# A two-layer language-model tower on one core: the recurrence's 8-column products streamed four times over

## What is computed

```
def _rnn_layer(inp, W_ih, W_hh, b_ih, b_hh):
    pre = jnp.einsum('bsi,hi->bsh', inp, W_ih) + (b_ih + b_hh)
    h0 = jnp.zeros((inp.shape[0], W_hh.shape[0]), dtype=inp.dtype)
    def step(h, p_t):
        h = jnp.tanh(p_t + h @ W_hh.T)
        return (h, h)
    _, hs = jax.lax.scan(step, h0, jnp.swapaxes(pre, 0, 1))
    return jnp.swapaxes(hs, 0, 1)
...
h = _rnn_layer(x, W_ih_0, W_hh_0, b_ih_0, b_hh_0)
h = _rnn_layer(h, W_ih_1, W_hh_1, b_ih_1, b_hh_1)
return h @ fc_w.T + fc_b
```

## Time and profile before

| what | value |
|---|---|
| median of 3 runs | 1154.31 us (1153.18 to 1155.77) |
| span of the profiled execution | 1152.6 us |
| PE busy | 1094.6 us, 95% |
| PE weight loads busy | 935.8 us, 81% |
| ACT busy | 787.2 us, 68% |
| DVE busy | 699.3 us, 61% |
| mean granted TensorE clock | 0.642 |
| L656, 8-column matmuls | 16384, 169 ns each |

### The profile page before, as it was taken

The page is one execution under the profiler, slowest core; times in us unless marked ns, Lnnn a source line. Parts: engine busy times, 40 slices in busy tenths (PEclk is TensorE's granted clock), DMA queues, the critical chain, the costliest instruction groups (busy, mean ns, idle before and its releaser), DMA issues.

```text
span 1152.6 us, 62476 instructions
## 1 busy us (share of the span) xinstructions
PE 1094.6 (95%) x26880; PEld 935.8 (81%) x26880; DVE 699.3 (61%) x3140; ACT 787.2 (68%) x4577; POOL 144.5 (13%) x220
## 2 busy tenths in 40 slices
PE   4799999999999999999999999999899879889998
PEld 2699999999999999999999999999744368823333
DVE  7565455555555555555555544444456769899996
ACT  1466777777777777777777777677567878666664
POOL 4200000000000000000000000000003302331210
PEclk9555555555555555555555555555599989999999
DMA  4000000000000000000000000000000000256686
GB/s 143 8 9 10 9 9 14 9 9 9 10 13 10 9 9 9 10 14 9 9 5 5 4 5 5 5 4 5 3 1 1 1 1 1 86 212 228 247 285 204
DMA packets 30594, 47.22 MB, mean 41 GB/s; under 512 B 12322, under 2 KB 21611, under 8 KB 30316
## 3 DMA queue, kind: packets, MB, share of 16 engines
q1 hardware_dynamic: 29772, 43.08, 11.2%
q10 hardware_dynamic: 544, 0.13, 0.0%
HBM read 40.84 MB, written 2.36 MB: 37 GB/s over the span
## 4 chain that ended last, share of the span: by engine, by line
PE 86%; DVE 5%; ACT 3%; POOL 2%; issue 2%; DMA 1%; SPq 1%; DVEq 0%; POOLq 0%; ACTq 0%
PE bank L656 44%; PE bank L752 7%; PE bank L1403 6%; PE bank L735 5%; PE bank L1708 5%; PE bank L426 4%; PE bank L525 3%; PE bank L730 2%; PE bank L1436 1%; PE bank L747 1%; PE bank L1585 1%; PE bank L411 1%; PE bank L446 1%; PE bank L315 1%; PE bank L1493 1%
## 5 line engine op out<-in xcount | busy, mean ns | idle before, releaser
L656 PE MATMUL bank<-space,whh_hi 128*128 128x8 f16 x16384 | 609.5, 169 | 7.4 <-DVE space L783 4.4
L656 PEld LDWEIGHTS bank<-space,whh_hi 128*128 128x128 f16 x16384 | 528.4, 105 | 25.3 <-DVE space L783 7.4
L783 DVE TENSOR_TENSOR space<-h_f,space 128x16 f16<-128x16 f32 x2048 | 291.5, 176 | 380.4 <-ACT h_f L764 378.8
L764 ACT ACTIVATE h_f<-bank 128x16 f32<-128x16 f32 x2048 | 300.1, 184 | 229.8 <-PE bank L656 222.4
L770 ACT ACTIVATE space<-bank 128x16 f16<-128x16 f32 x2048 | 299.0, 184 | 1.1 <-PE bank L656 1.1
L656 PE MATMUL bank<-space,whh_lo 128*128 128x32 f16 (+1 forms) x2096 | 145.0, 190 | 0.0
L752 PE MATMUL bank<-space,wih_hi 128*128 128x32 f16 x2048 | 137.1, 188 | 0.0
L426 PE MATMUL bank<-onehot,tab 128*128 128x128 f16 x448 | 116.7, 266 | 0.5 <-DVE prepare_cur L476 0.5
L735 PE MATMUL bank<-xr,wih_hi 128*128 128x32 f16 x512 | 109.8, 214 | 0.0
L730 PE MATMUL bank<-ones,bias 128*128 128x32 bf16 x512 | 102.9, 201 | 0.0
L656 PEld LDWEIGHTS bank<-space,whh_lo 128*128 128x128 f16 x2096 | 102.2, 107 | 0.0
(11 more groups left out here) (303 smaller groups left out, 1637.8 us busy)
## 6 DMA issues: line engine op xcount, KB each, us to landing
space<-weights_kept SPq DMA_DIRECT2D x64, 512.0 KB, 7.7
space<-in_x SPq DMA_DIRECT2D x28, 129.0 KB, 3.1
out<-res SPq DMA_DIRECT2D x7, 256.0 KB, 9.9
space<-in_wrec SPq DMA_DIRECT2D x1, 768.0 KB, 4.1
space<-in_wx SPq DMA_DIRECT2D x1, 740.5 KB, 9.0
brec<-in_brec SPq DMA_DIRECT2D x1, 260.0 KB
ew<-in_ew SPq DMA_DIRECT2D x1, 256.0 KB, 4.1
weights_kept<-wturned SPq DMA_DIRECT2D x8, 32.0 KB, 1.8
```

The source lines that it names most:

```text
L656: mm = pe.matmul(own[:, m, :], w[:, k, m * P:(m + 1) * P], steps(h, k), start=False, stop=False, skip_group_check=True)
L764: act.activation(h_f[layer][:, s % 2, :, :], own, ACT.Tanh, scale=scale[layer]).then_inc(s_h[layer], 1)
L783: dve.tensor_tensor(h[layer][:, :, s % RINGS[layer], 1, :], h_f[layer][:, s % 2, :, :], h[layer][:, :, s % RINGS[layer], 0, :], ALU.subtra ...
```

## The change

The four matmuls of each state product stream 32 columns in place of 8. The moving operand is the same 8 columns four times, read with a step of zero. The output goes to the 8 columns of the step's own sums and to three copies of them, at distances of 64, 128 and 192 columns in the same bank, which nothing reads. The products with `whh_lo`, the inputs, biases and all other matmuls are as before.

```diff
@@ -27,6 +27,7 @@
 OFF = 2 * U + 2
+COPIES = 4
 EPS = 1e-5
@@ -106,6 +107,11 @@
             return bank[layer * 3 + block % 3][:, 0:KH * U * B].rearrange("p (m s b) -> p m s b", m=KH, b=B)
+
+        def wide_sums(layer, s):
+
+            own = bank[layer * 3 + s // U % 3].rearrange("p (j m s b) -> p m s j b", m=KH, s=U, b=B)
+            return own[:, :, s % U, 0:COPIES, :]
@@ -657,14 +663,23 @@
             return mm
 
+        def add_wide(pe, own, w, state):
+
+            for m in range(KH):
+                for k in range(KH):
+                    mm = pe.matmul(own[:, m, :, :], w[:, k, m * P:(m + 1) * P],
+                                   state[:, k, :].unsqueeze(1).to_broadcast([P, COPIES, B]),
+                                   start=False, stop=False, skip_group_check=True)
+            return mm
+
         def rec_tensor(pe, g):
 
             def low(layer, s):
                 if 0 <= s < T:
                     pe.wait_ge(s_lo[layer], OPEN + s)
                     at = (s - 1) % RINGS[layer]
-                    add(pe, sums(layer, s // U)[:, :, s % U, :], whh_hi[layer], h[layer],
-                        lambda h, k: h[:, k, at, 1, :]).then_inc(s_sum[layer], 1)
+                    add_wide(pe, wide_sums(layer, s), whh_hi[layer],
+                             h[layer][:, :, at, 1, :]).then_inc(s_sum[layer], 1)
@@ -672,8 +687,8 @@
                     pe.wait_ge(s_hi[layer], OPEN + s)
                     at = (s - 1) % RINGS[layer]
-                    add(pe, sums(layer, s // U)[:, :, s % U, :], whh_hi[layer], h[layer],
-                        lambda h, k: h[:, k, at, 0, :]).then_inc(s_part[layer], 1)
+                    add_wide(pe, wide_sums(layer, s), whh_hi[layer],
+                             h[layer][:, :, at, 0, :]).then_inc(s_part[layer], 1)
```

## The result

The changed kernel takes **1140.85 us** (median of 4 runs, 1140.43 to 1142.36) against 1154.61 us before (4 runs): a ratio of 0.9882, with a 95% interval of 0.9868 to 0.9896. It is 1.2% faster. The forecast was 1136, with a range of 1126 to 1155. The span of its profiled execution, which took 1142.36 us and was the slowest of the four, is 1140.4 us. In what follows, one run of the kernel without L735 that took 1314.4 us, at a granted clock of 0.52 in place of 0.64, is left out of the figures.

A forecast was written before the change was run, and what follows sets the result against it. Main bound: the recurrence's 753 ns low loop, with PE's stream second. At 2.4 GHz, 1033 × (765.3 − 746) = 19.9 us, less 1.5, took the span from 1152.6 to 1134.2; plus 1.7, 1136 us, range 1126 to 1155.

The forecast's parts named there:

- The low loop: Recurrence's closed loop: four low-state products, tanh, subtraction, products again; claimed as main bound, about 753 ns a step.
- the stream: PE's sequence of products and filled-in matmuls in a recurrence step; claimed to cost 0.012 us a step, some 12 us.
- The clock: PE's granted clock in the recurrence; claimed to rise from 1.2 to 2.4 GHz soon after layer 1 starts and stay.
- the slower rival: Recurrence clock stays at 1.2 GHz, wider products add only latency: loop 773 ns, time 1168 us; chance 0.13.
- The loop at the high clock: Low-state product, tanh and subtraction loop at 2.4 GHz: claimed 746 ns a step, bounds 734 and 764.
- the first weight load: Load opening each burst of low products, at most 27 ns; claimed to halve at 2.4 GHz, −12 ns, bounds 0 and −13.
- The remainder of 1.5: Allowance of 1.5 us in all for waits at the recurrence's start, where the preparation holds up some steps.
- The signs that I named: Profile after: clock at 9 or 10 tenths, products at 176 ns, steps of 0.75, PE's subtraction waits among the longest.
- The layout rival: Copies' spaced output and zero-step operand cost two cycles a column: loop 763 ns, time 1153 us, no change; chance 0.06.
- the larger gain: Last matmul of a burst ends 10 ns earlier at 2.4 GHz: loop 728 ns, time 1117 us; chance 0.03.

## Why the prediction was right

**The bound, as read: right.** The low loop is 753.4 ns before and 750.5 after, and the stream stretched some steps above it: a third of that was taken away by itself in a run, and all of it went with the high clock. Split by the trace, the recurrence's 13.1 us are 1033 × (753.4 − 750.5) = 3.0 us of the loop and 1033 × (11.9 − 2.2) = 10.0 us of what lay above it. The larger part came from the smaller of the two bounds, since little of the loop depends on PE's clock. Three readings of the chain were loose and change nothing: the step at 405.37 has L735 three times and L747 twice, not L735 twice and L747 once, and the step at 404.64 has 7 matmuls behind its products and takes 0.73, that at 403.89 has 9.

**The clock: right, and decisive.** It rose at 49.1 us and stayed until 810.3. The steps ahead of that and the last ones ran at the low level with 32 columns, most of them at 773 to 774 ns, which is the loop the slower rival had. It also fell and rose again at the end of the recurrence, as foreseen. The forecast gave this 0.78 on an argument about how fully the array is fed; the outcome bears it out for these products, and the kernel with 16 columns shows that a smaller change would have missed.

**The loop at the high clock: the term that was mis-sized.** I had 746 and it is 750.5, so that of a forecast gain of 7 ns a step in the loop only 3 came. (The sum itself was off by one: 753 less 8 is 745, which would have made the forecast 1135.) By its parts: the gaps between the four matmuls went from 27 to 25 (−5 in all; −4 foreseen), the last matmul from 168 to 176 (+8; +8 foreseen), and the signals to and from DVE took 1 ns more each, with the tanh and the subtraction 1 ns less each. The wrong one is the first weight load. I let it halve, from about 24 to 12. The first matmul of a burst takes 190 against 176 for the others and starts 4 behind its load, so it is 18: −6 in place of −12. With that and the 1 ns more from the gaps my 746 would have been 751, and 745 would have been 750. The 4.5 ns a step are 4.6 us of the 4.85 that the forecast was short. The rest nearly cancels: 2.3 us lay above the loop where I had left 1.5, the part outside the recurrence grew by 0.9, and the median stands only 0.5 above the profiled span, where I had 1.7, because the profiled execution was 1.5 slower than the median. The remainder of 1.5 rested on a sum that is off as well: 16 × 25.6 and 12 more matmuls make 0.72 us, not under 0.70, which is still below the loop.

**The signs that I named: one was wrong.** I expected PE's waits for the subtraction to appear among the longest. They do not; in the list of waits for 200 to 700 us the two rows have hardly changed (ahead of them, before and after, stands only GpSimd, waiting for VectorE in the preparation of later tokens):

```profile
DVE space L798 <- ACT h_f L779: 224.5, 645, 0.7
ACT h_f L779 <- PE bank L670: 132.9, 518, 0.5
```

PE's share of the chain stayed at 86% too. A matmul of 25 ns of array time is shown with 176, so gaps of 0.1 us stay covered by matmuls in flight. It was the idle time before the weight loads that grew, from 25.3 us in all to 74.8:

```profile
L656 PEld LDWEIGHTS bank<-space,whh_hi 128*128 128x128 f16 x16384 | 528.4, 105 | 25.3 <-DVE space L783 7.4
...
L670 PEld LDWEIGHTS bank<-space,whh_hi 128*128 128x128 f16 x16384 | 487.9, 96 | 74.8 <-DVE space L798 8.7
```

**The rivals.** The slower one had its price right, as far as the low stretches of the kernel with wide low products show it, and its condition was not met. The layout rival and the larger gain did not occur: 176 ns is what the rows of before gave for 32 columns. The Trainium skill's formulas for a single matmul (TensorE: Matmul & The Clock Gate, Single matmul latency) would have had it fall from 189 to 179, an estimate; the trace has the last matmul of a burst, the one that counts, rise from 168 to 176. The first matmul of a burst does take 188 with 8 columns at 1.2 GHz, near the formula, but 190 with 32 at 2.4 GHz.

## What to carry to other kernels

Ask of every matmul on a dependent path how its latency and its pace change with the columns, at both levels of the clock, and put extra columns where no one waits for them: widening the high products alone, to 64 columns and in nine steps of 32 to 32, gave 1132 us where widening all gave 1141. Before counting on a higher clock, find the loop and split it by engine; here three fifths of the step lay on ACT, DVE and the signals between the engines, which kept their times to within 1 ns each when PE's clock doubled. The change gave 1.2%, the best kernel 2.0%. And try several sizes of such a change and look at the granted clock of each: half of it was a loss (1160 us), and twice of it one as well (1175 us).

## What the runs showed that I had not expected

The first weight load of a burst, taken as the way to the fourth matmul less three gaps, does not halve with the clock: 105 − 81 = 24 ns at 1.2 GHz, 93 − 75 = 18 at 2.4. Small matmuls go at 25 ns each at 2.4 GHz for 8 columns and for 32, where at 1.2 GHz they go at 27 for both, so the doubled clock gives such a stream only some 7%. The Trainium skill (TensorE: Matmul & The Clock Gate, Part 1) has the 25 ns as a floor between the starts of small matmuls; these runs agree. The doubled clock gives more to the few that hold the array longer: two of L735 took 0.11 us in the chain before and two of L750, its successor, 0.07 after; one of 128 columns 0.11 and 0.07.

The clock can change levels dozens of times in one kernel while the work repeats: with wide low products only, 458 steps began at one level and 575 at the other. A mean clock between 0.5 and 1 over a stretch (0.77 there) was such a mixture, and the time was no better than at the low level throughout. What makes it rise and fall was not measured; these runs show it for their own products and give no rule.
